# Earlier loads of the first head pair's Q and K, with the alibi tiles placed ahead of them in SBUF

## The reference

```python
xn  = layernorm(x)                         # 2048 x 1024, no gain or bias
qkv = xn @ W_attn + b_attn                 # 1024 x 3072; 16 heads of 64
att = q k^T / sqrt(64) / temperature
att = att + slope[h] * (key - query)       # alibi; -inf above the diagonal
y   = softmax(att) @ v
h   = silu(xn @ wg.T) * (xn @ wu.T)        # int32 weights / 127, 3072 wide
out = x + y @ W_proj + b_proj + h @ wd.T
```

## Time and profile before

| | us |
|---|---|
| timed runs | 2059.57 and 2079.99, median 2069.78 |
| profiled execution | 2057.46 |
| its span, from the first to the last instruction of the slowest core (core 4) | 2055.9 |
| spans of the eight cores | 2042.6 to 2055.9 |

### The profile page before, as it was taken

One profiled execution on the slowest core, in us unless ns is written; L12 is line 12 of the kernel. 1 busy time (PEld: TensorE's weight loads), 2 busy tenths in 40 slices (PEclk: granted clock), 3 DMA queues, 4 the chain that ended last, 5 costly groups with the idle time before them and its releaser, 6 DMA issues.

```text
span 2055.9 us, 26119 instructions; the slowest of 8 cores (2042.6 to 2055.9 us)
## 1 busy us (share of the span) xinstructions
PE 1334.6 (65%) x8564; PEld 696.2 (34%) x8642; DVE 947.0 (46%) x1601; ACT 923.0 (45%) x1745; POOL 79.2 (4%) x148
## 2 busy tenths in 40 slices
PE   0000049899899898269985666565656565666766
PEld 0000024344344343124433334343434443433333
DVE  2334221011010110144208878797878787855563
ACT  2334333023031130000127877878878777853442
POOL 0010000000000000013100000000000000000000
PEclk9999999999999999679995555555555555566778
DMA  8877544244152341532203100001010102002112
GB/s 259 279 257 239 171 155 145 101 131 156 45 181 103 123 156 50 179 138 75 90 21 103 47 16 29 35 6 58 1 62 1 62 1 72 1 21 82 62 62 93
DMA packets 46188, 198.87 MB, mean 97 GB/s; under 512 B 6119, under 2 KB 6120, under 8 KB 38378
## 3 DMA queue, kind: packets, MB, share of 16 engines
q1 hardware_dynamic: 31978, 148.96, 22.3%
q0 software_dynamic: 14080, 48.24, 6.4%
HBM read 157.34 MB, written 39.85 MB: 96 GB/s over the span
## 4 chain that ended last, share of the span: by engine, by line
PE 51%; DMA 14%; DVE 12%; issue 11%; ACT 11%; DVEq 0%; ACTq 0%; POOL 0%; SPq 0%; POOLq 0%
PE ps_dn L404 8%; PE ps_g L360 8%; PE ps_u L368 8%; PE ps_tr L774 8%; DVE snegp L662 6%; PE ps_qk L490 5%; ACT ptb L738 5%; ACT pbuf L698 4%; PE ps_y L799 4%; PE ps_tr L874 3%; PE ps_v L526 3%; DVE ncmx L624 2%; PE ps_s L643 2%; DMA wistage<-wd_r 2%; DMA wst<-wattn 2%
## 5 line engine op out<-in xcount | busy, mean ns | idle before, releaser
L774 PE MATMUL ps_tr<-ident_s,pbuf 128*128 128x128 bf16 x2176 | 287.2, 293 | 215.6 <-ACT ytile L817 112.7
L662 DVE SCALAR_TENSOR_TENSOR snegp<-ps_s,abcp 128x1024 f32<-128x1024 f32 (+2 forms) x320 | 330.1, 1056 | 190.8 <-PE ps_s L649 190.8
L738 ACT ACTIVATE ptb<-ps_tr 128x512 bf16<-128x512 f32 (+3 forms) x640 | 313.5, 531 | 229.5 <-PE ps_tr L774 224.8
L624 DVE TENSOR_REDUCE ncmx<-snegp 128x2 f32<-128x1024 f32 (+2 forms) x320 | 328.2, 1051 | 3.5
L698 ACT ACTIVATE pbuf<-snegp,negmax 128x128 bf16<-128x128 f32 (+15 forms) x256 | 305.1, 1194 | 36.4 <-DVE negmax L679 34.8
L774 PEld LDWEIGHTS ps_tr<-ident_s,pbuf 128*128 128x128 bf16 x2176 | 189.0, 126 | 330.3 <-issue 320.7
L643 PE MATMUL ps_s<-k_hp,q_hp 64*128 64x512 bf16 (+2 forms) x320 | 140.1, 497 | 100.9 <-DVE snegp L662 94.7
L404 PE MATMUL ps_dn<-wdres,hbuf 128*128 128x512 bf16 x752 | 176.4, 392 | 36.8 <-DVE xfout L425 30.5
L294 PE MATMUL ps<-ident_s,xn_st 128*128 128x128 bf16 x128 | 16.2, 305 | 263.7 <-DVE xn_st L277 263.7
L360 PE MATMUL ps_g<-xnT,wgbuf 128*128 128x512 bf16 x752 | 181.4, 381 | 9.1 <-DMA wubuf<-wu_sc 8.3
L376 ACT ACTIVATE gs_s<-ps_g 128x512 bf16<-128x512 f32 x96 | 57.3, 597 | 276.5 <-PE ps_g L360 269.6
(11 more groups left out here) (65 smaller groups left out, 984.6 us busy)
## 6 DMA issues: line engine op xcount, KB each, us to landing
wgbuf<-wg_sc SPq DMA_DIRECT2D x48, 512.0 KB
wubuf<-wu_sc SPq DMA_DIRECT2D x48, 512.0 KB
abcp<-alibi_bc SPq DMA_DIRECT2D x16, 1024.0 KB
wistage<-wg_r SPq DMA_DIRECT2D x12, 1024.0 KB
wistage<-wu_r SPq DMA_DIRECT2D x12, 1024.0 KB
wistage<-wd_r SPq DMA_DIRECT2D x12, 1024.0 KB
wst<-wattn SPq DMA_DIRECT2D x8, 1536.0 KB
xstage<-xin SPq DMA_DIRECT2D x16, 512.0 KB
```

The costliest lines, as they stand in the source:

```text
L624: cd = S.op("vector", lambda e, par=par, sp=sp, c0=c0, w=w, ci=ci: e.tensor_reduce(ncmx[:, par * 8:par * 8 + 8].rearrange("p (j c) -> p j ...
L662: stt = S.op("vector", lambda e, sp=sp, hb=hp % 2, aoff=aoff, c0=c0, w=w, rA=rA: e.scalar_tensor_tensor(snegp[sp].rearrange("p (j t) -> p ...
L738: return e.activation(dst, src, AF.Copy)
L774: lasttr = S.op("tensor", lambda e, par=par, j=j, kc=kc, slot=slot, idx=idx, n=len(kcs): e.matmul(ps_tr[:, slot * 512 + (kc % 4) * 128: sl ...
```

## The change

The q_hp load of the early call waits for the converted weights and for the last two stores of q_sc[0] and of k_sc[0], and no longer for all stores and the last matmul of V. The k_hp load has no list of its own before or after. The two alibi tiles are allocated ahead of q_hp and k_hp, abcp1 first. The order in which DMAs are issued stays as it is, and so do all other instructions.

```diff
                 if early:
                     wts = [wat_fin, qk_st_war[2], qk_st_war[3]]
-                    wq = qk_st_fin + [("pe", p3_pe)]
+                    wq = [wat_fin] + store_of_fc[0] + store_of_fc[8]
...
             outsb = E4b(nc.sbuf_tensor("outsb", [128, C], F32, side="right"))
+            abcp1 = E4b(nc.sbuf_tensor("abcp1", [128, 2 * T], F32, side="right"))
+            abcp0 = E4b(nc.sbuf_tensor("abcp0", [128, 2 * T], F32, side="right"))
+            abcp = [abcp0, abcp1]
             q_hp = [E4b(nc.sbuf_tensor(f"q_hp{i}", [128, T], BF16, side="right")) for i in range(2)]
             k_hp = [E4b(nc.sbuf_tensor(f"k_hp{i}", [128, T], BF16, side="right")) for i in range(2)]
-            abcp = [E4b(nc.sbuf_tensor(f"abcp{i}", [128, 2 * T], F32, side="right")) for i in range(2)]
```

## The result

| | before | changed |
|---|---|---|
| median of all runs, us | 2059.56 (42 runs) | 2056.23 (43 runs) |
| ratio to the kernel before | | 0.9981, 95% interval 0.9971 to 0.9990 |
| span of the slowest core in the profiled execution, us | 2055.9 (core 4) | 2053.4 (core 7) |

A fifth of a per cent is gone: 2059.56 x 0.0019 = 3.9 us, between 2.1 and 6.0 by the interval. The forecast, 2052 us within 2045 to 2076, and the same kernel by the 2% bound, holds. The forecast gain of 5.35 us lies inside the interval, near its far end.

The account below looks back on a forecast made before the run. The slowest core, core 4 (2055.9 us), set the time, with late q_hp and k_hp loads on its path between V and attention. Sum: 2057.46 - 5.35 = 2052.1 us, other terms nothing; range 2045 to 2076.

Parts of the forecast that it names:

- The forecast gain of 5.35 us: Passage from V to attention: scores start at 1074.36 instead of 1079.71 us, and nothing comes back; chance 0.80.
- The late loads were the gap: At the end of V, q_hp and k_hp cost 5.58 us; issued at 1016 they land by 1022 us, hidden.
- The next thing late is ScalarE's copy: First score matmul then waits for ScalarE's copy of the last V bank, ending 1074.22, plus 0.14 us of issue.
- The forecast idle stretch of 0.8 us: TensorE's gap between V and the first scores: 6.18 - 5.35 = 0.8 us.
- Order on SP, places of tiles, loads under V: nothing: Earlier queued loads, moved abcp tiles and SBUF writes during V cost nothing; the last at most 0.15 us.
- The shift goes to the end: Attention has no appointment at a fixed time, so the 5.35 us pass through, give or take 1.6.
- a scatter of 1.6 us: Allowance on the 5.35 us passing through attention to the end.
- a sign of being right: Attention: 926 to 928 us from first to last score matmul on every core.
- rival C: First scores of attention: the shorter gap keeps TensorE's clock up, 1.8 us more gained, 2050.3 us; chance 0.08.
- The sentence that a clock up all through attention would give little more: From 1200 to 1500 us, clock 0.52 on core 2, 0.60 on core 6; core 6 slower, 927.2 against 926.0 us.

Follow-up runs that it names:

- the second profile without the wait: Changed kernel with the first score matmul no longer waiting for ScalarE's last copy of V, run a second time; ratio 0.9987 to the kernel before.
- The double load: Kernel with new tile places but the old q_hp wait, plus q_hp and k_hp of the first head pair each loaded twice; ratio 1.0034 to the kernel before.
- the same ten profiles: The ten profiles of this study, over its several kernels, of which all cores are read, 80 cores; no single time or ratio.

## Why the prediction was right, point by point

**The late loads were the gap.** Right. Undoing the wait alone brought the gap back (5.93 us) and the ratio to 0.9999, and the loads left where the working put them: landed by 1020 us against a forecast 1022. The new waits never held SP.

**The next thing late is ScalarE's copy.** Right in kind, 0.35 us off in size. From the end of a landing to the matmul I had read 0.14 us; behind ScalarE it was 0.49, the issue in the chain of the changed kernel. In the kernel before, k_hp was the last of the first score matmul's waits to be met. Now ScalarE's semaphore is the first of the four that stand ahead of that matmul in the code. That it is ScalarE that is slow to be heard doesn't fit: in the second profile without the wait, on core 3, only 0.14 us lie between the end of one of its copies at 1931.91 and the transpose that waited for it. That the other three waits are stepped through one by one fits the difference, but no run shows it. So core 4's own gap fell from 6.6 to 1.6, that is by 5.0 us instead of 5.35, and the eight cores' by 4.7, because core 4 had one of the longer gaps: they were 5.8 to 6.7. The forecast idle stretch of 0.8 us was 1.20.

**Order on SP, places of tiles, loads under V: nothing.** Right. wpj_b left at 1073.10, 1.2 us behind the start of the last V matmul; head pair 1 had its K issued 74 us before the alibi tile of pair 0 was let go; additions at 1218 ns with the moved abcp1; V matmuls at 379.

**The shift goes to the end.** Right for some 70 to 80% of it. The double load shows that a shift isn't swallowed (4.5 us of gap, 4.4 of time, the last tenths by luck). But pairs 0 to 6 became 1.0 us longer, and with the gap's 4.7 that leaves 3.7, beside 3.2 and 3.8 in the two profiles and 3.9 in the timed runs. The forecast had put nothing here beyond a scatter of 1.6 us. It had named 926 to 928 us from first to last score matmul on every core as a sign of being right and a longer attention as one of being wrong. Measured were 928.0 to 929.4, so this sign spoke against it: the time came out near the forecast although one of its terms, nothing comes back, was off by a microsecond.

**The clock, rival C.** Its sign was wrong. The shorter gap didn't keep the clock up. The clock fell to 0.50 near 1076.0 us before, 2.9 us behind the start of the last V matmul on core 4, and near 1074.5 in the changed kernel, 2.6 us behind it on core 7 (the 0.63 in 1074 to 1076 us). Over the eight cores the fall came 2.2 to 5.0 us behind it before and 2.5 to 5.6 after. The first scores merely start ahead of the fall now. That bought almost nothing: from the first score matmul to the first transposes it took 4.15 us before and 1077.57 - 1073.47 = 4.10 after, because VectorE and ScalarE set that stretch, a table load of 1.28 us on ScalarE included. What the clock took was later. In pairs 0 to 6 it fell from 0.551 to 0.535. Behind its fall at the end of V it was up again for a first time within 58 us of the last V matmul on five of eight cores before, and in the two profiles of the changed kernel on none of sixteen before 60.5 us. Over the same ten profiles the length of pairs 0 to 6 on a core falls by 0.55 us for each 0.01 of clock in it (80 cores, correlation -0.82); 0.016 make 0.9 us, nearly the whole of what came back. A correlation doesn't show which way the cause runs, and no run set the clock.

**Where the argument failed.** The sentence that a clock up all through attention would give little more. It set core 6 at 0.60 against core 2 at 0.52 and found core 2 quicker over the whole of attention. The whole was the wrong distance to compare: core 2 was the one core with the short step in its last pair (202.5 us, the others 206.1 to 206.4; 2.8 of the 3.7 us are that step). Over pairs 0 to 6 core 6 took 731.2 us and core 2 733.7, as their clocks say. One event worth 3.7 us hid a dependence that was in the profile from the start.

**What stays open.** That the start of attention decides where the clock steps up is supported by what came back in each second profile (0.50 to 0.52 on sixteen of sixteen cores with a gap of 1.6 us; 0.55 or more on fifteen of sixteen with 0.3; both kinds side by side with 4 to 9 us), but no run set the clock by itself, and no row says what places the steps up.

## What to carry to other kernels

A load that stands on the path once is worth about its own length, once: look at the chain at a change of stage, find the wait ahead of it in the issuing queue, and ask whether it is there for the data or only for the memory that the tile shares. Early data are worth more than the gap that they close: with Q and K at hand most of the first step's latency went behind V, which gave another 3.9 us. A wait put down to shared memory is worth checking against the allocations: that of the first scores on ScalarE guarded nothing and cost 1.3 us. Before a scatter between cores is used as a bound, split it by stage and by step; effects of a few microseconds of both signs can add up to a quiet total.

## What the runs showed of the hardware that I had not expected

The granted clock of TensorE in a stage that doesn't keep it busy went with when the stage starts. A start some 1.3 us earlier against the end of V (gap 0.3 for 1.6 us) went with a clock of 0.56 for 0.54 in the first seven head pairs and with 1.8 us less time, in both profiles of each kernel. And a single stretch of 16 projection matmuls ran at 379 or at 631 ns each, 3 us of a step, with a granted clock of 0.86 or 0.60 in that step and the same work on the other engines.

The same matmul started 0.14 us behind what released it where that was the last of its four waits in the code, and 0.47 to 0.50 us behind it where that was the first and the others had long been met (0.49 in the chain of core 7; sixteen cores). What takes the difference is not shown.
